# Moving gather-and-add edge units to earlier stages of a graph and attention kernel

## The reference, cut to what matters

```python
xn = layernorm(x)                                   # 6250 nodes x 256
gnn = segment_sum(edge_weight[:, None] * xn[dst], src, 6250)   # 100000 edges
x = x + gnn + mix(xn)                               # mix: attention with a polynomial kernel, 8 heads of 32
x = x + moe(layernorm(x))                           # 16 experts, top 2, then a layernorm

# mix: moments of the keys, once over all nodes, then every query reads them
kv_mod = einsum('bhni,bhnj,bhne->bhije', kn, kn, vN)
kv     = einsum('bhnd,bhne->bhde', kn, vN)
y = 0.5*einsum('bhni,bhnj,bhije->bhne', qn, qn, kv_mod) + scale**2*einsum('bhnd,bhde->bhne', qn, kv) + scale**4*vsum
out = (y[..., 1:] / y[..., :1]) @ Wproj.T + bproj
```

## Time and profile before

| | |
|---|---|
| median of three runs | 2761.56 us |
| profiled execution / its span | 2775.81 us / 2774.0 us |
| key turns with edge units, steady part (603.60 to 1050.79 us) | 447.19 us for 34 turns |
| query halves of full width (1085.01 to 1934.66 us) | 849.65 us for 24 halves |
| behind the last half (from 1950.81 us) | 823.09 us |
| busy in the span: PE / DVE / POOL | 2037.9 / 1663.6 / 1318.4 us |

### The profile page before, as it was taken

The page is one execution under the profiler, slowest core; times in us unless marked ns, Lnnn a source line. Parts: engine busy times, 40 slices in busy tenths (PEclk is TensorE's granted clock), DMA queues, the critical chain, the costliest instruction groups (busy, mean ns, idle before and its releaser), DMA issues.

```text
span 2774.0 us, 43029 instructions
## 1 busy us (share of the span) xinstructions
PE 2037.9 (73%) x12138; PEld 1345.3 (48%) x12139; DVE 1663.6 (60%) x4163; ACT 692.3 (25%) x1826; POOL 1318.4 (48%) x1239
## 2 busy tenths in 40 slices
PE   4656756788888887788878888788553899999400
PEld 2444543454454554444444444344543899999400
DVE  6999998788888886444544445344434332323367
ACT  2301111111111111222222222222321344444333
POOL 1274443677777775556656556554355000000375
PEclk8668878899999999899989889888555999999755
DMA  4300001222222222222322222237722333333333
GB/s 164 116 31 24 25 26 23 76 80 80 80 81 81 79 81 65 74 83 87 90 75 87 80 81 89 76 80 73 282 74 99 97 106 105 107 104 106 102 119 119
DMA packets 147101, 243.44 MB, mean 88 GB/s; under 512 B 27873, under 2 KB 104931, under 8 KB 146948
## 3 DMA queue, kind: packets, MB, share of 16 engines
q0 software_dynamic: 55488, 149.11, 19.7%
q1 hardware_dynamic: 88500, 89.91, 10.2%
q10 hardware_dynamic: 2960, 2.55, 0.3%
HBM read 190.08 MB, written 51.38 MB: 87 GB/s over the span
## 4 chain that ended last, share of the span: by engine, by line
PE 35%; another core or an unknown queue 7%; issue 7%; DVE 5%; POOL 3%; DMA 2%; ACT 1%; DVEq 1%; SPq 1%; ACTq 0%; POOLq 0%
PE bank L1938 7%; PE bqk L1958 7%; PE b L1698 7%; PE bank L1815 4%; PE bqk L1826 3%; PE b L1710 2%; POOL big L738 2%; DMA big<-xn_dram,big 1%; POOL big L707 1%; PE bank L1898 1%; DVE acc L1242 1%; DVE big L1232 1%; DVE big L1449 1%; PE bqk L1862 1%
## 5 line engine op out<-in xcount | busy, mean ns | idle before, releaser
L707 POOL DMA_INDIRECT big<-xn_dram,big x880 | 918.0, 1043 | 545.1 <-PE b L1698 212.3
L1698 PE MATMUL b<-big 128*128 128x256 f32 x1760 | 537.6, 434 | 84.5 <-DVE acc L1242 37.1
L1698 PEld LDWEIGHTS b<-big 128*128 128x128 f32 x1760 | 339.5, 211 | 329.3 <-issue 178.1
L1242 DVE TENSOR_TENSOR acc<-acc,b 128x256 f32 x440 | 183.7, 418 | 371.6 <-remote 178.1
L738 POOL DMA_INDIRECT big<-y_dram,idxz x100 | 111.7, 1117 | 492.2 <-issue 484.3
L1232 DVE TENSOR_SCALAR big<-big 128x128 f32<-128x128 f32 x880 | 299.0, 361 | 7.5 <-DVE big L1282 7.0
L1938 PEld LDWEIGHTS bank<-late,mid 128*128 128x128 f32 x1872 | 228.9, 193 | 7.3 <-DVE mid L1566 1.4
L864 ACT ACTIVATE big<-bank 128x512 f32<-128x512 f32 (+1 forms) x208 | 104.7, 577 | 506.8 <-remote 209.8
L1938 PE MATMUL bank<-late,mid 128*128 128x128 f32 x1872 | 229.7, 276 | 1.1 <-DVE mid L1566 1.1
L1958 PE MATMUL bqk<-big,mid 128*128 x928 | 219.5, 380 | 0.0
L1575 DVE TENSOR_TENSOR mid<-bqk,mid 128x256 f32<-128x256 f32 x116 | 49.3, 425 | 242.8 <-PE bqk L1958 242.8
(11 more groups left out here) (318 smaller groups left out, 3059.5 us busy)
## 6 DMA issues: line engine op xcount, KB each, us to landing
big<-w SPq DMA_DIRECT2D x8, 2048.0 KB
mid<-z_dram SPq DMA_DIRECT2D x120, 128.0 KB, 2.2
mid<-b SPq DMA_DIRECT2D x118, 128.0 KB, 3.0
y_dram<-mid SPq DMA_DIRECT2D x116, 128.0 KB, 1.7
big<-xn_dram,big POOLq DMA_INDIRECT x880
acc<-x_pad SPq DMA_DIRECT2D x10, 640.0 KB, 6.0
xn_dram<-big SPq DMA_DIRECT2D x10, 640.0 KB, 3.4
y_out<-big SPq DMA_DIRECT2D x10, 640.0 KB
```

The source lines that it names most:

```text
L707: pool.indirect_dma_start(out=gx[t % EB], out_offset=None, in_=xn_dram, in_offset=bass.IndirectOffsetOnAxis(ap=dstA[:, t:t + 1], axis=0)). ...
L1242: v.tensor_tensor(mine, mine, ps_pair[p % 2][:, 0:C], ALU.add).then_inc(s_add, 1)
L1698: a = pe.matmul(ps_pair[p % 2][:, 0:C], wd[t % (2 * EB)], gx[t % EB], start=(j == 0), stop=(j == 1))
```

## The change

Five units instead of four stand in each key turn from turn 6 on, so the key turns carry 215 instead of 172. A query half carries fourteen instead of eleven until the list ends: halves 0 to 15 have fourteen each, half 16 has one, and halves 17 to 25 have none. Before, halves 0 to 23 had eleven and the last two halves two each. At each `next_edge` place up to two units now stand instead of one. The second projection of a batch keeps its place behind the first `next_edge`.

```diff
-KE = 4
+KE = 5
 KP = (NK - SKIP) * KE
 EP = 440
-PER = 11
+PER = 14
+SLOT = 2
 def first_edge(z):
-    if z >= 2 * NQB:
-        return EP
-    if z >= 2 * (NQB - 1):
-        left = EP - KP - 2 * PER * (NQB - 1)
-        return EP - left + (z % 2) * (left // 2)
-    return KP + PER * z
+    return min(EP, KP + PER * z)
 def pair_order():
-            mine.insert(2, ("proj", QB * (z // 2 - 1) + 2))
+            mine.insert(1 + min(SLOT, len(mine) - 1), ("proj", QB * (z // 2 - 1) + 2))
 # in query_half, on DVE and on PE alike
                 def next_edge():
-                    e = next(go, None)
-                    if e is not None:
-                        edge(e)
+                    for _ in range(SLOT):
+                        e = next(go, None)
+                        if e is not None:
+                            edge(e)
```

## The result

The kernel after takes 2797.58 us (median of four runs, 2796.17 to 2800.18) against 2763.64 us of the kernel before beside it (four runs, 2752.27 to 2771.3): 1.012 times, with an interval of 1.009 to 1.015. It is slower by more than the 0.5% that a measurement can tell. The forecast was 2760 us; the measured time lies in the range given and on the side that got 0.47.

The account below looks back on a forecast made before the run. The prediction took DVE to bound the key turns and a loop of waits the query halves, POOL second busiest in both. Terms +73, -71 and -4 gave -2 us, taken off 2761.56: 2760 us, 8-in-10 range 2655 to 2865.

Parts of the forecast that it names:

- the side that got 0.47: Whole kernel: the outcome slower than before, given 0.47 against 0.36 for faster and 0.17 for the same.
- the second bound: Key turns: POOL's ten gathers at the bare 1.25 us each need 14.45 us a turn, above DVE's 13.99.
- the key turn hides the stretch: Second rival, key turns: the gathers' stretch shrinks and DVE sets 13.99 us, +36; sum -39, 2722 us; chance 0.09.
- the lock in full: Key turns: no gather proceeds beside DVE's products, 17.4 us a turn, +183; sum +108, 2870 us; chance 0.05.
- the third rival: Another name for the lock in full: key turns of 17.4 us, 2870 us in all, chance 0.05.
- the present tails: Query halves: 23 seven-unit stretches from a half's fifth collection onward; one near the middle, 20.65 us, gave 41.2 for fourteen units.
- The first rival: The spread relieves the queue: POOL runs through, halves 36.0 us, key turns 14.45; sum -102, 2660 us; chance 0.18.
- late releases: Query halves: PE's finished results become known late when POOL issues gathers back to back; such waits total 209.8 us on ACT.
- the steps that I put at 12.9: Halves without units: PE's selections, answers and fourth group's squares sum to 12.9 us a half; eight halves 118, taken as 120.
- The fourth rival: Late releases in both stages: key turns 15.85 us, +116, halves 43.8; sum +83, 2845 us; chance 0.26.
- the term of -71 us for the 24 halves: Query halves: the 24 full halves go from 849.65 to 659 + 120 = 779 us, -71.
- the two halves of the change nearly cancel: Whole kernel: key turns +73, full halves -71 and last two halves -4 sum to -2 us.

Follow-up runs that it names:

- e2: Kernel before with fourteen units in a half, two per place, key turns left at four units: 2807.4 us, 1.015 of before.
- e4: Changed kernel with one semaphore count per group of four selections or four answers instead of one per matmul: 2803.4 us, 1.014 of before.
- e10: The changed kernel, unedited, on a chip without remote waits: 2649.8 us, 1.026 of before.
- e1: Kernel before with five units in each key turn, halves still ten at one per place: 2732.0 us, 0.986 of before.
- e3: Kernel before with four units in a key turn and eleven in a half, but two at a place: 2777.0 us, 1.002 of before.
- e5: Changed kernel without the 450 gathers of the halves, so the graph part is not computed in full: 2511.5 us.
- e8: Six units in a key turn, eight in a half at one per place, against the kernel before: 2573.0 us, 0.994.
- e16: Five units in key turns, the halves' 225 units spread evenly over 24 halves, plus an ineffective padding edit, against the kernel before: 2537.3 us, 0.981.
- e11: Five units in a key turn, ten in a half at one per place, on a chip without remote waits: 2555.8 us, 0.990 of before.
- e9: The kernel before, unchanged, on a chip without remote waits: 2587.7 us profiled, 2580.4 us in the median beside it.
- e6: Changed kernel with the halves' gathers fetching 64 floats a row instead of 256, graph part not computed in full: 2650.4 us.
- e17: e16 with padding edges meant to name rows 49 apart, though they still named row 0: 2536.2 us, 0.981 of the kernel before.

## Why the prediction was wrong, step by step

**The key turns** were right: 14.92 us in the mean, forecast 14.85, +69 for 42 turns against +73 for 43. POOL is the bound there, not DVE: the steady gathers are 359.62 / 319 = 1.127 us long, plus 0.30, ten are 14.3 us, and the steady median is 14.64. Without remote waits the steady turn is 14.44, the bare 14.45 of the second bound. I had looked for POOL at 9 tenths in the slices; they show 7, and the forecast's test should have counted the gaps. The rivals "the key turn hides the stretch" (13.99) and "the lock in full" (17.4) fall on both kinds of chip. Single gathers do come near a lock (the one at 832.76 lost 0.74 us with 0.88 of the products left), but over the stage ten gathers lose 10 x (1.127 - 0.95) = 1.8 us a turn beside 4.9 us of products. The Trainium skill (SBUF - State Buffer, "Who interferes with whom") calls the shared port pair an exclusive lock. Read as the third rival reads it, that no gather proceeds beside a product, it would give the 17.4; the trace agrees in kind only.

**The fourteen-unit halves** came out at 41.8 us, forecast 41.2: 668.6 against 659, +10. The way to the number, the present tails, held on that chip (e2: 42.3, e4: 42.4). The first rival, 36.0 us in a half that POOL runs through, fell there; on the chips without remote waits it is what happens, 35.0 us in fourteen of sixteen halves. So the reading of the earlier trace rows as late releases was of use, but the cause that I gave it, POOL's unbroken streaks, is not shown: 336 gathers in a row made nothing late in e10. Nor do the readers move only once POOL has stopped. Worked out from the starts and ends in the trace of after, ACT began a square more than 1 us after its inputs' recorded ends and its own last instruction 40 times in these halves, 105 us in all, and in 18 of the 40 POOL had made no pause over 0.6 us in between. The number came out because its source, the tails, had the same late releases in them, whatever makes them.

**The halves without units** were mis-sized: 15.85 and 16.8 us in turn, 130 for eight, against 120. The clock was 1.00, as I had taken it; a pair of them took 32.65 us where the terms gave 2 x 12.9 + 3.7 = 29.5. PE's records fill nearly all of it (129.55 of 129.96 us), so the steps that I put at 12.9 were too short as work of PE rather than for a wait:

```profile
1825.87:1955.83 129.96, 129.55 (x678) 47.77 (x679) 50.98 (x48) 72.78 (x145) 0.00 (x0) 1.00 0.00 1
```

This failure is of the size alone, +10 us.

**The smaller terms**: the moments' stretch grew by 2.7 us, which had no term; the last two halves and all behind them gave +0.3 instead of -4.

**The sum.** Against the profiled execution: forecast -2, measured +21.5. The difference of 23.5 is 10 + 10 from the halves, -4 from the key turns, and 7.5 from the small terms (2.7, 4.3 and 0.5 ahead of turn 6). The other 14 us are the basis: I took off 14 for a profiled execution above its median, and the one of after lies at its own. The fourth rival, +83 us from late releases in both stages, was the nearest in sign only: its key turn (15.85) did not come, and 2798 lies between forecast and it.

So the failing step is the term of -71 us for the 24 halves, which measured -51, and behind it the sentence "the two halves of the change nearly cancel". They are of opposite sign. The key part alone gains 1.4% (e1), and what turns it into a loss is emptying eight halves: 742.8 us with ten in each of 22 halves, 798.6 with fourteen in sixteen; two at a place cost nothing by themselves (e3). I priced that by rows and never asked what the same units would cost if spread.

What explains it on the chips without remote waits is a half that takes the longer of two: POOL's 2.5 us a unit, or PE's 16.3 us with no unit and 0.79 more for each ((27.35 - 16.3) / 14, from e5). Worked out from these, and beside them the measured means (e5, e8, e16, e11, e9 and e10, without the halves of the slow end):

| units in a half | POOL | PE | measured |
|---|---|---|---|
| 0 | 0 | 16.3 | 16.3 |
| 8 | 20.0 | 22.6 | 22.0 |
| 9.4 | 23.4 | 23.7 | 24.0 |
| 10 | 25.0 | 24.2 | 25.8 |
| 11 | 27.5 | 25.0 | 29.0 |
| 14 | 35.0 | 27.4 | 35.0 |

The longer of the two is met within 0.6 us, but for ten and eleven units, where the halves are 0.8 and 1.5 us longer. PE's line is an estimate, drawn between its two ends. The lines cross between nine and ten units. Below that a unit costs a half 0.8 us, above it 2.5 us. Fourteen and none cost (35.0 + 16.3) / 2 = 25.7 a half for seven units in the mean, where two halves of seven would take PE's 21.8 each. That is why even spreading (e16) is best, and why five units in the key turns, which bring the halves to 9.4, gain. On the chip with remote waits the loss by emptying halves is there too, at a higher level: 16.3, 32.2, 35.4, 41.8 us for 0, 10, 11 and 14, so that fourteen and none cost 29.1 a half in the mean. Where the lines cross there was not measured: only single halves of one, two or five units ran on it.

**What stays open**: what makes releases late. In the same kernel a half of fourteen takes 41.8 us with them and 36.4 without, and before's 24 halves 850 and 710 us. On the chip that has them they accompany the DMAs that GpSimd issues. The halves without units show none. Behind the halves, in the trace of before, they come back where POOL issues scatters about 1.27 us apart (line 716, 1970 to 2148 us):

```profile
ACT late L886 <- remote: 24.3, 6, 8.8
```

And between 2150 and 2600 us, where POOL issues nothing, ACT waits for PE 119 times and DVE 116 times, and no wait is remote. That speaks against counts of PE that come late whatever GpSimd does. Why the other chips show nothing of it, with the same gathers, is not known; the experiments that were to tell (pauses, no gathers) ran on those. Also open is the slow end of the list.

## What to carry to other kernels

When work of one engine is dealt out over stages, work out for each stage the longer of the two engines as a function of how much it gets, and fill every stage to the point where the lines cross; emptying a stage in which the dealt engine then idles is a loss, however well the rest is packed. Before reading a wait as a mechanism, look whether it is there on another chip: the same file took 2765 and 2585 us here. And test an edit of data where it arrives, since a table that is read in another type can leave the experiment void without a sign in the time.

## What the runs showed of the hardware

- A gather of 128 rows from GpSimd costs its engine 1.25 us (0.95 and 0.30 between), and costs the same at 256 bytes a row as at 1024: 36.4 us a half in the mean for both (e6, e10).
- The same kernel ran at 2761 to 2765 us on some chips and at 2580 to 2587 on others. Of before's difference 139 us lie in the 24 halves and 38 us behind them (839.3 against 801.2), and only 4 in the key turns.
- Readers of PE's results started several us after the matmul's recorded end on one kind of chip, and never more than 0.9 us after it on the other (ACT's squares in the full halves: 40 times over 1 us in after, 23 times in before, none in e9 and e10; matmul ends in the trace are modelled). One of them in after: the selections end at 1502.73, POOL goes on issuing, and ACT starts 5.8 us later. The 15.14 us of idle time are mostly from before that end:

```profile
1501.59 1.14 PE L1812 MATMUL bank<-big 32*128 32x512 f32 x8
...
1508.08 0.95 POOL L703 DMA_INDIRECT big<-xn_dram,big  x1 [0.30 <-issue]
...
1508.49 0.60 ACT L860 ACTIVATE big<-bank 128x512 f32<-128x512 f32 x1 [15.14 <-remote]
```

- The gathers of the list's last units, padding blocks by the count above, kept the DMA engines busy for 0.92 of the time at 78 GB/s, where others took 0.36 at 103 GB/s (e11). On the other chips looked at it is alike: 0.78 at 77 GB/s in e1, 0.97 at 78 in e17.
